# Written-out rounds, a skip term on TensorE and new instruction lists in a hybrid state-space and attention kernel

## What is computed

```python
x = x + ssm(layernorm(x))      # state-space block
x = x + local(layernorm(x))    # two layers of local attention and feed-forward
x = x + power(layernorm(x))    # attention with squared scores and decay
x = x + local(layernorm(x))    # the same two layers again

# ssm, for one sequence
x = resid * rsqrt(mean(resid**2) + eps) * norm_w
xs = silu(conv(x @ in_w.T) + conv_b); skip = x @ skip_w.T
delta = softplus(xs @ wd1.T @ wd2.T + wd2_b); B, C = xs @ wb.T, xs @ wc.T
h = exp(delta * A) * h + (delta * xs) * B      # over the tokens, 16 states
y = sum_n(h * C) + xs * W_D
return resid + (y * silu(skip)) @ out_w.T
```

## Time and profile before

| | |
|---|---|
| median of 3 runs | 3252.09 us (3251.75 to 3260.75) |
| the profiled execution | 3256.39 us |
| its span, first to last instruction | 3254.3 us |
| granted TensorE clock, mean | 0.950 |
| busy, share of the span | PE 84%, DVE 77%, ACT 69%, POOL 41% |
| state-space rounds | about 30 to 600 us |
| local attention, first and second call | about 629 to 1602 and 2271 to 3244 us |
| power attention | about 1625 to 2240 us |

### The profile page before, as it was taken

One profiled execution on the slowest core, in us unless ns is written; L12 is line 12 of the kernel. 1 busy time (PEld: TensorE's weight loads), 2 busy tenths in 40 slices (PEclk: granted clock), 3 DMA queues, 4 the chain that ended last, 5 costly groups with the idle time before them and its releaser, 6 DMA issues. The chain is left out here.

```text
span 3254.3 us, 63725 instructions
## 1 busy us (share of the span) xinstructions
PE 2733.6 (84%) x18784; PEld 1833.6 (56%) x18784; DVE 2491.6 (77%) x3831; ACT 2250.4 (69%) x5987; POOL 1345.4 (41%) x1073
## 2 busy tenths in 40 slices
PE   4888888489999999999588899896799998999996
PEld 2444444256666666666367777674466665666664
DVE  6999999767777777777468777877677777777774
ACT  4788788256667666666378888885476666666664
POOL 4666666444455454555300000001454544554542
PEclk9999999789999999999689999998899999999998
DMA  2000000000000000000000000000000000000000
GB/s 85 1 0 0 0 0 0 0 1 0 0 0 0 11 12 0 0 0 10 11 1 2 1 1 1 1 1 1 1 0 0 0 0 11 12 0 0 0 0 26
DMA packets 17099, 15.66 MB, mean 5 GB/s; under 512 B 3998, under 2 KB 14943, under 8 KB 16863
## 3 DMA queue, kind: packets, MB, share of 16 engines
q1 hardware_dynamic: 16958, 14.19, 1.5%
HBM read 12.09 MB, written 2.10 MB: 4 GB/s over the span
## 5 line engine op out<-in xcount | busy, mean ns | idle before, releaser
L920 POOL TENSOR_TENSOR f_p<-f_p,f_rs 128x512 f32<-128x512 f32 (+1 forms) x256 | 320.8, 1253 | 755.2 <-DVE f_rs L869 755.2
L765 ACT ACTIVATE f_p<-pair,f_nm 128x128 f32<-128x128 f32 (+1 forms) x1024 | 389.0, 392 | 231.3 <-DVE f_nm L858 230.6
L912 POOL TENSOR_TENSOR f_qb<-f_kn,f_tab 128x512 f32<-128x512 f32 x256 | 444.5, 1758 | 193.5 <-DVE f_kn L838 193.5
L561 POOL TENSOR_TENSOR m_hc<-m_h,m_c 128x512 f32<-128x512 f32 x256 | 325.2, 1291 | 187.1 <-DVE m_h L523 155.2
L523 DVE TENSOR_TENSOR_SCAN m_h<-m_a,pair 128x1024 f32<-128x1024 f32 x128 | 292.1, 2282 | 17.6 <-DVE pair L516 12.1
L719 PE MATMUL bank<-f_hnT,f_w 128*128 128x256 f32 (+1 forms) x768 | 217.5, 407 | 83.4 <-DVE f_u L895 77.8
L637 PE MATMUL pair<-f_wqkv,f_hT 128*128 128x512 f32 x512 | 261.0, 633 | 11.2 <-DVE f_kn L838 9.1
L680 PE MATMUL pair<-ident,f_p 128*128 128x128 f32 x1536 | 245.5, 283 | 29.0 <-POOL f_p L920 26.7
L421 PE MATMUL bank<-m_hc,ident 128*128 128x512 f32 x512 | 256.8, 644 | 14.3 <-POOL m_hc L561 14.2
L1174 POOL TENSOR_TENSOR X<-X,p_y 128x256 f32 (+1 forms) x16 | 11.6, 726 | 618.7 <-DVE p_y L1168 618.7
L828 DVE TENSOR_REDUCE f_ss<-f_sq 128x16 f32<-128x1024 f32 x128 | 155.2, 1212 | 140.2 <-ACT f_sq L736 140.1
(11 more groups left out here) (181 smaller groups left out, 6563.1 us busy)
## 6 DMA issues: line engine op xcount, KB each, us to landing
f_wqkv<-in_f_wqkv SPq DMA_DIRECT2D x4, 768.0 KB, 4.0
X<-in_x SPq DMA_DIRECT2D x16, 128.0 KB, 2.6
out_x<-X SPq DMA_DIRECT2D x16, 128.0 KB, 2.0
f_w<-in_f_w SPq DMA_DIRECT2D x4, 341.0 KB, 3.5
f_wo<-in_f_wo SPq DMA_DIRECT2D x4, 256.0 KB, 2.7
sel<-in_sel SPq DMA_DIRECT2D x1, 768.0 KB
f_w<-in_f_w SPq DMA_DIRECT2D x4, 192.0 KB, 3.3
p_wqk<-in_p_wqk SPq DMA_DIRECT2D x1, 512.0 KB
```

Source lines behind the costliest of these rows:

```text
L561: op = nc.gpsimd.tensor_tensor(m_hc[:, g % 4, n], m_h[:, g % 2, n], m_c[:, g % 2, n].unsqueeze(1).broadcast_to([P, EC, L]), ALU.mult)
L765: op = nc.scalar.activation(f_p[:, t, j, k0:k1], SC[:, j, k0:k1], ACT.Exp, bias=f_nm[:, t, j:j + 1], accum_out=f_sm[:, t, j:j + 1])
L912: op = nc.gpsimd.tensor_tensor(f_qb[:, t, :, o].rearrange("p (x h) d -> p x h d", x=2), f_kn[:, t, :, 32 - 32 * e:64 - 32 * e].rearrange(" ...
L920: op = nc.gpsimd.tensor_tensor(f_p[:, t, :, k0:k1], f_p[:, t, :, k0:k1], f_rs[:, t, :].unsqueeze(2).broadcast_to([P, 4, k1 - k0]), ALU.mult)
```

## The change

1. `run_windows` and `run_layers` have no loop any more. Every round is written out, and every wait has a constant value.
2. In the state-space block the step `ys` is gone. `y7` on PE, which ends the sum over the states, adds two products of a diagonal matrix `m_skip` (W_D on the diagonal) with xs; `yg` reads the sum from PSUM. `xr` moves from DVE to ACT and drops the constant factor, which goes into `m_nw`, the scaled `norm_w` that `xTe` uses.
3. In several steps of that block the waits stand in another order.
4. The lists and lags of the state-space block and of local attention are new; those of power attention are not.

```diff
-    odd = (count - n + 1) % 2
-    for k in range(1, n + odd):
-        window(k, k % 2, range(min(k, n)))
-    with eng.Fori(0, (count - n + 1) // 2) as p:
-        for b in range(2):
-            window(2 * p + (n + odd + b), (n + odd + b) % 2, range(n))
-    for k in range(count + 1, count + n):
-        window(k, k % 2, range(k - count, n))
+    for k in range(1, count + n):
+        window(k, k % 2, [lag for lag in range(n) if 1 <= k - lag <= count])
...
 F_STAGES = [
     "zc xT hT qk0 v0 sq0 ve0 v1 ve1 ss0 cl0 lr0 rn0 kn0 qa0 qb0 qs0 qk1 sq1 ss1 cl1 lr1 rn1 kn1 qa1 qb1 qs1 "
-    "T00 Te00 T01 Te01 T10 T11 Te10 Te11 p00",
-    "s00 nm00 rs00 pT000 pe000 o00 s10 nm10 p10 rs10 pn10 pT100 pe100 pT101 pe101 o10 oe0 s01 nm01 p01 rs01 "
-    "pn01 pT010 pe010 s11 nm11 p11 rs11 pn11 o01 pT110 pe110 pn00",
-    "wo z1 sh hb st mv rv hn hnT he w1a g0 w1b g1 u1 w1c u0 w2 z2 pT111 o11 oe1 pe111 zb vv"]
+    "T00 T01 T10 T11",
+    "s00 nm00 p00 rs00 pT000 pe000 o00 s10 nm10 p10 rs10 pn10 pT100 pe100 pT101 pe101 o10 s01 nm01 p01 rs01 "
+    "pn01 pT010 s11 nm11 rs11 Te10 Te11 Te00 Te01 pn00",
+    "wo z1 sh hb st mv rv hn hnT he w1a g0 w1b g1 u1 w1c u0 w2 z2 o01 pT110 pT111 o11 pe110 oe1 pe111 p11 "
+    "pe010 oe0 pn11 zb vv"]
 F_ORDER = {
-    "dve": "zc hT nm00 pe111 ss0 rs00 cl0 nm10 kn0 z1 qa0 rs10 st nm01 mv qs0 hn ss1 cl1 rs01 pe101 kn1 nm11 qa1 u1 "
-        "qs1 u0 rs11 z2",
-    "pe": "xT s00 pT111 qk0 o11 s10 wo pT000 v0 sh s01 qk1 o00 v1 s11 pT100 T00 hnT pT101 T01 w1a o10 pT010 w1b w1c "
-        "o01 T10 w2 T11 pT110",
-    "act": "sq0 oe1 lr0 rn0 p10 hb pe000 ve0 p01 sq1 ve1 pe100 Te00 he lr1 rn1 g0 oe0 pe010 Te01 g1 p11 Te10 Te11 "
-        "pe110 p00",
-    "pool": "pn00 qb0 vv rv pn10 pn01 qb1 zb pn11"}
+    "dve": "zc hT nm00 pe111 rs00 ss0 cl0 nm10 z1 kn0 st mv rs10 nm01 qa0 hn ss1 rs01 cl1 qs0 kn1 qa1 u1 nm11 pe101 "
+        "u0 qs1 rs11 z2",
+    "pe": "pT110 o01 xT s00 pT111 qk0 o11 s10 wo v0 sh s01 qk1 pT000 v1 hnT s11 w1a pT100 w1b T00 pT101 o00 w1c T01 "
+        "pT010 w2 T10 o10 T11",
+    "act": "Te00 p11 Te01 pe010 Te10 oe0 Te11 pe110 p00 sq0 oe1 lr0 rn0 p10 hb ve0 sq1 p01 pe000 lr1 he rn1 g0 ve1 "
+        "pe100 g1",
+    "pool": "pn11 pn00 zb qb0 vv rv pn10 pn01 qb1"}
...
 M_ORDER = {
-    "dve": "bx5 h5 r1 bx6 delta h6 lo bx7 xr h7 bx0 h0 bx1 ys h1 yg bx2 h2 x bx3 h3 ue bx4 h4",
-    "pe": "bC7 y4 y5 bB0 bC0 xT bB1 bC1 y6 y7 xe bB2 bC2 out skip bB3 bC3 u bC4 bB4 y0 y1 bB5 z bB6 bC5 bc bC6 y2 y3 "
-        "bB7",
-    "act": "a0 xTe c0 a1 sq c1 a2 xs c2 a3 c3 a4 gate a5 c4 abs c5 exp hi a6 ln mid2 c6 c7 mid a7",
-    "pool": "hc0 hc1 hc2 me hc3 rr hc4 hc5 dx hc6 xx hc7"}
+    "dve": "bx1 h1 bx2 yg h2 bx3 h3 ue bx4 x h4 bx5 h5 r1 bx6 delta h6 lo bx7 h7 bx0 h0",
+    "pe": "bB7 bB0 y4 bB1 bC0 y5 y6 bC1 y7 bB2 xT bC2 bB3 xe bC3 skip bB4 u bB5 out bc bC4 z bC5 y0 bB6 y1 bC6 y2 y3 "
+        "bC7",
+    "act": "xTe sq c2 a3 xs c3 gate a4 c4 a5 abs c5 exp hi ln a6 mid2 a7 c6 mid a0 c7 a1 c0 xr a2 c1",
+    "pool": "dx hc6 xx hc7 me rr hc0 hc1 hc2 hc3 hc4 hc5"}
...
                 for n in range(GN):
                     mm = nc.tensor.matmul(bank[1][:], ident[:], m_hc[:, g % 4, n].rearrange("p c l -> p (c l)"),
-                                          start=g == 0 and n == 0, stop=g == NG - 1 and n == GN - 1)
+                                          start=g == 0 and n == 0, stop=False, skip_group_check=True)
+                if g == NG - 1:
+                    for c in range(EC):
+                        mm = nc.tensor.matmul(m_y_ps[:, c, :], m_skip[:, c, :], m_xs[:, b, c, :], start=False,
+                                              stop=c == EC - 1, skip_group_check=True)
...
+            elif s == "xr":
+                act.wait_ge(*pe_m.at(i - 1, "xT"))
+                act.wait_ge(*pool_m.at(i, "rr"))
+                for t in range(T):
+                    op = nc.scalar.activation(m_xr[:, t, :], tiles(seq(Z, z_at))[:, t, :], ACT.Copy, scale=m_rr[:, t:t + 1])
...
             elif k == "h":
+                dve.wait_ge(*m_before(pool_m, i, "hc", g, 2))
+                dve.wait_ge(*act_m.at(i, f"a{g}"))
                 dve.wait_ge(*dve_m.at(i, f"bx{g}"))
-                dve.wait_ge(*act_m.at(i, f"a{g}"))
-                dve.wait_ge(*m_before(pool_m, i, "hc", g, 2))
...
-            elif s == "ys":
+            elif s == "yg":
+                dve.wait_ge(*pe_m.at(i - 1, "out"))
                 dve.wait_ge(*pe_m.at(i, f"y{M_LAST}"))
-                for c in range(EC):
-                    op = nc.vector.scalar_tensor_tensor(out=m_y[:, c, :], in0=m_xs[:, b, c, :], scalar=mw["W_D"][:, c:c + 1],
-                                                        in1=m_y_ps[:, c, :], op0=ALU.mult, op1=ALU.add)
-            elif s == "yg":
-                dve.wait_ge(*dve_m.at(i, "ys"))
-                dve.wait_ge(*pe_m.at(i - 1, "out"))
-                op = nc.vector.tensor_tensor(m_yg[:], m_y[:], m_gate[:, b], ALU.mult)
+                op = nc.vector.tensor_tensor(m_yg[:], m_y_ps, m_gate[:, b], ALU.mult)
...
+            nc.vector.tensor_scalar(m_nw[:], mw["norm_w"][:], float(D) ** 0.5, None, ALU.mult).then_inc(const_set, 1)
+            for c in range(EC):
+                op = nc.vector.tensor_scalar(m_skip[:, c, :], ident[:], mw["W_D"][:, c:c + 1], None, ALU.mult)
+            op.then_inc(const_set, 1)
```

More of the change, by code:

```diff
@@ L164, in window @@
                 step(s, layer, k - lag - layer * count, (parity - lag) % 2)
[L166 to L176, removed]
+    for k in range(1, 2 * count + n):
+        window(k, k % 2, [lag for lag in range(n) if 1 <= k - lag <= 2 * count], lambda lag: int(k - lag > count))
 def build(nc, ins, out):
@@ L289, in build @@
         m_hc = m_sb("m_hc", [P, 4, GN, EC, L])
-        m_y = m_sb("m_y", [P, EC, L])
+        m_skip = m_sb("m_skip", [P, EC, P])
+        m_nw = m_sb("m_nw", [P, 1])
         m_yg = m_sb("m_yg", [P, EC, L])
@@ L380, in m_pe @@
             if s == "xT":
-                pe.wait_ge(*dve_m.at(i, "xr"))
+                pe.wait_ge(*act_m.at(i, "xr"))
                 pe.wait_ge(*dve_m.at(i - 1, "lo"))
@@ L416, in m_pe @@
             elif k == "y":
-                pe.wait_ge(*pool_m.at(i, f"hc{g}"))
                 if g == 0:
                     pe.wait_ge(*dve_m.at(i - 1, "x"))
+                pe.wait_ge(*pool_m.at(i, f"hc{g}"))
                 for n in range(GN):
                     mm = nc.tensor.matmul(bank[1][:], ident[:], m_hc[:, g % 4, n].rearrange("p c l -> p (c l)"),
-                                          start=g == 0 and n == 0, stop=g == NG - 1 and n == GN - 1)
+                                          start=g == 0 and n == 0, stop=False, skip_group_check=True)
[3 more added lines that the diff above has]
+                                              stop=c == EC - 1, skip_group_check=True)
             elif s == "out":
@@ L437, in m_act @@
                                               accum_out=m_ss[:, t:t + 1])
+            elif s == "xr":
[3 more added lines that the diff above has]
+                    op = nc.scalar.activation(m_xr[:, t, :], tiles(seq(Z, z_at))[:, t, :], ACT.Copy, scale=m_rr[:, t:t + 1])
             elif s == "xTe":
+                act.wait_ge(const_set, 17)
+                act.wait_ge(*pe_m.at(i - 1, "skip"))
                 act.wait_ge(*pe_m.at(i, "xT"))
-                act.wait_ge(*pe_m.at(i - 1, "skip"))
-                op = nc.scalar.activation(m_xT[:, CONV - 1:], m_xT_ps, ACT.Copy, scale=mw["norm_w"][:])
+                op = nc.scalar.activation(m_xT[:, CONV - 1:], m_xT_ps, ACT.Copy, scale=m_nw[:])
             elif s == "gate":
@@ L448, in m_act @@
                 act.wait_ge(*pe_m.at(i, "xe"))
-                act.wait_ge(*dve_m.at(i - 2, "ys"))
+                act.wait_ge(*dve_m.at(i - 2, "yg"))
                 for c in range(EC):
@@ L481, in m_act @@
             elif k == "c":
+                act.wait_ge(*m_before(pool_m, i, "hc", g, 2))
                 act.wait_ge(*pe_m.at(i, f"bC{g}"))
-                act.wait_ge(*m_before(pool_m, i, "hc", g, 2))
                 op = nc.scalar.activation(m_c[:, g % 2], m_bcast(g, 1), ACT.Copy)
@@ L488, in m_dve @@
             k, g = s.rstrip("0123456789"), int("0" + s[len(s.rstrip("0123456789")):])
-            if s == "xr":
-                dve.wait_ge(*pool_m.at(i, "rr"))
-                dve.wait_ge(*pe_m.at(i - 1, "xT"))
-                for t in range(T):
-                    op = nc.vector.tensor_scalar(m_xr[:, t, :], tiles(seq(Z, z_at))[:, t, :], m_rr[:, t:t + 1],
-                                                 float(D) ** 0.5, ALU.mult, ALU.mult)
-            elif s == "ue":
+            if s == "ue":
                 dve.wait_ge(*pe_m.at(i, "u"))
@@ L512, in m_dve @@
             elif k == "bx":
+                dve.wait_ge(*pool_m.at(i, "dx"))
                 dve.wait_ge(*pe_m.at(i, f"bB{g}"))
-                dve.wait_ge(*pool_m.at(i, "dx"))
                 dve.wait_ge(*m_before(dve_m, i, "h", g, 1))
@@ L543, in m_pool @@
```

(6 more changed lines are left out.)

## The result

The change takes 3225.8 us (median of 4 runs, 3222.5 to 3226.7) beside 3254.4 for the kernel before: a ratio of 0.991 (95% interval 0.989 to 0.9925), 28.6 us less. The forecast was -44, so the sign came out and the size fell short by 15 us.

A forecast was written before the change was run, and what follows sets the result against it. VectorE bounds the state-space stage, TensorE's queue local attention, ScalarE power attention's short rounds, with back-edge stalls in long ones. Power attention -49, state-space -50, local attention +55: -44, so 3208 us against the median; range 3140 to 3268.

The forecast's parts named there:

- Steps 4 and 5: Local attention: qb0 holds qa0, which holds vv until 13.0; rv ends at 13.8; pn10 goes first, hn ends at 15.6.
- steps 6 and 7: Local attention, TensorE: waits 2.4 us for hnT behind hn, then 0.4 for he, which stands behind lr1.
- The three waits: Local attention, TensorE: 2.4 for hnT, 0.4 for he, 0.7 for g0, together 3.5 us a round.
- The clock: Local attention: TensorE's waits lower its granted clock, +0.4 a round on average, from 29.3 to 29.7.
- Step 8: Local attention: g0, after its gelu table load, ends at 19.9, so TensorE waits 0.7 us more.
- the sum of its gaps: State-space stage: VectorE's idle time a round, 1.1 for five product-scan pairs and 0.5 for short waits.
- The edges: State-space stage's edges: took its gain from -48 to -50 us.
- Written out, but fetched late: Rival: straight code makes engines wait like the back edge, power attention gains nothing; +5, 3257 us; chance 0.09.
- Not held: Rival, local attention: vector and POOL instructions miss each other, hn ends at 13.4, round 27.5; 3085 us; chance 0.08.
- The slower clock case: Rival, local attention: low clock lasts through w1c, round 31.2, 3292 us; chance 0.16 including the stretch from 30.5.

The follow-up runs named there:

- the first experiment: Kernel before with its rounds written out and nothing else, old lists, steps and waits kept: 3154.6 us, ratio 0.969.

## Why the prediction was right, and where it was off

*Power attention* was right to a microsecond: 34.40 us twice in a row, 13 intervals in 447.3 against 447.2. The first experiment gives the same with nothing else changed, so it is the loop that made the long rounds. That late instructions were the means was read from the idle time put down to "issue" and was not tested apart from the loop's other costs.

*Local attention* was right in mechanism, step by step. Steps 4 and 5 are shown each by the run that takes its cause away, and the waits of steps 6 and 7 came as 2.38 and 0.39 for 2.4 and 0.4. The sum, 29.7 a round against 29.67, came out so closely by luck: two errors of opposite sign nearly cancel. At the full clock a round takes 28.9, not 29.3. The three waits come to 2.37, 0.43 and 0.69 in the full-clock round shown above, 3.5 as summed; it is TensorE's own work that is smaller, 25.37 us with the new list for the 25.84 taken from the old one, for a reason that was not followed. The clock, taken as +0.4, is worth 0.78. Step 8's 0.7 appears at the full clock and is hidden when w1a runs slowly, since then g0's table is loaded beside it.

*The state-space stage* is where the forecast was off: 32.23 a round for 31.6. The term that was mis-sized is VectorE's work, and not the sum of its gaps. The gaps are (451.20 - 427.35) / 14 = 1.70 a round, for 1.6 forecast, but that they agree is luck, as they are of another make: ten of 0.13 and not five of 0.22. The forecast had no term for the new order of waits, and it gave writing out nothing in this stage, where the first experiment shows almost 1 us a round. The work is 427.35 / 14 = 30.53, for 30.0. I had priced xr at 1.96 from the earlier trace rows. The table by line in the kernel before, over nine rounds, has

```profile
L493 DVE TENSOR_SCALAR m_xr<-Z,m_rr 128x128 f32 x18 | 12.5, 735 | 0.0
```

which is 1.39 a round: the row in time (1.96) was of one of the rounds in which both halves ran beside instructions of POOL. yg cost nothing more in reading PSUM (0.68 for 0.67), and TensorE, at 398.16 / 14 = 28.4 a round for the 30.0 forecast, did not come near to being the bound. Table loads fell from two pairs to one as forecast.

*The edges* cost +4.5 us, where -2 stood for them. The forecast had no term for how the new lists fill and drain.

*The rivals.* "Written out, but fetched late" is refuted by the first run. "Not held" did not happen, but the runs that took the holds away show what it was worth: a round of 27.75, close to the 27.5 worked out for it. The slower clock case came in seven of the 56 rounds (30.75) and not on the mean.

The prediction missed a comparison that the experiments made plain. It set the new list against the looped round. Against its own written-out predecessor the new list loses 87 us, not 55.

## What to carry over

Price a change of an instruction list against the same list in the new surroundings, not only against the kernel as it is; writing the rounds out was worth 100 us here and the list that came with it cost about 90. Where VectorE and GpSimd both work on SBUF, follow who asks first: one wait that makes the non-urgent instruction yield (pn10 behind hn) gave 2.7%, and u1 (0.48 us) put ahead of qa1, which let qb1 go first, came with a loss of 57 (3107.2 + 57 - 14 = 3150, where 14 are the own waits' gain), some of it by the clock. Take the price of an instruction from the mean of its group when it can be held, and where, in written-out code, an instruction waits for the one before it on its own engine and for others, ask the own wait first.
